# Causal attention and gated MLP: seven PSUM banks as one ring with a bank a turn, exps of 512 columns, and new orders of TensorE's work

## What is computed

```python
qkv = x @ w_qkv                                  # x: (8, 512, 128)
q, k, v = jnp.split(qkv, 3, axis=2)              # 16 heads of 8
att = jnp.einsum('bhtd,bhsd->bhts', q, k) / np.sqrt(D)
att = jnp.where(causal, att, -jnp.inf)
att = jax.nn.softmax(att, axis=-1)
out = jnp.einsum('bhts,bhsd->bhtd', att, v)
x = _layernorm(x + out)
h = jax.nn.silu(x @ wg.T) * (x @ wu.T)
x = _layernorm(x + h @ wd.T)
```

## Time and profile before

| what | value |
|---|---|
| median of 3 runs | 353.14 us (351.8 to 357.61) |
| the profiled execution's own time | 353.12 us |
| its span (first to last instruction) | 351.4 us |
| busy: PE, DVE, ACT, POOL | 95%, 84%, 61%, 51% of the span |
| mean granted clock of TensorE | 0.989 of full speed |

### The profile page before, as it was taken

One profiled execution on the slowest core, in us unless ns is written; L12 is line 12 of the kernel. 1 busy time (PEld: TensorE's weight loads), 2 busy tenths in 40 slices (PEclk: granted clock), 3 DMA queues, 4 the chain that ended last, 5 costly groups with the idle time before them and its releaser, 6 DMA issues. The chain is left out here.

```text
span 351.4 us, 9106 instructions
## 1 busy us (share of the span) xinstructions
PE 333.8 (95%) x2947; PEld 197.1 (56%) x2947; DVE 294.0 (84%) x1251; ACT 214.7 (61%) x277; POOL 178.4 (51%) x325
## 2 busy tenths in 40 slices
PE   7799999999999999999999999999999998999990
PEld 3444464556556555645564565456455544798980
DVE  7979778898899889889898998899898974867765
ACT  3402567777767768677777777776677784333320
POOL 8400334734654474357445534843434469787633
PEclk9999989999999999999999999999999999999997
DMA  5797242554265327624541653185100010002021
GB/s 155 288 296 250 62 123 64 197 171 123 62 245 174 109 73 261 168 73 169 198 121 34 245 147 110 41 288 165 49 2 5 5 34 1 3 30 62 30 62 60
DMA packets 33903, 41.75 MB, mean 119 GB/s; under 512 B 3136, under 2 KB 17472, under 8 KB 33856
## 3 DMA queue, kind: packets, MB, share of 16 engines
q1 hardware_dynamic: 33696, 40.91, 36.7%
q10 hardware_dynamic: 160, 0.26, 0.2%
HBM read 21.76 MB, written 18.87 MB: 116 GB/s over the span
## 5 line engine op out<-in xcount | busy, mean ns | idle before, releaser
L903 DVE CUSTOM_DVE_ANT_0 masked<-psum,mask 128x384 bf16<-128x384 f32 (+3 forms) x512 | 218.9, 487 | 30.7 <-PE psum L490 26.5
L803 ACT ACTIVATE pt<-psum 128x1024 f32<-128x1024 f32 x160 | 158.4, 1021 | 51.8 <-PE psum L473 51.2
L1082 POOL TENSOR_SCALAR_AFFINE_SELECT pt<-pt 128x512 f32<-128x512 f32 x128 | 79.6, 634 | 95.7 <-ACT pt L803 93.9
L490 PE MATMUL psum<-kx,qx 33*128 33x384 f32 (+3 forms) x512 | 91.8, 354 | 1.6 <-DVE nm L903 0.7
L513 PE MATMUL psum<-pt,vx 128*32 128x256 f32 (+2 forms) x1280 | 92.1, 388 | 1.1 <-ACT oT L817 0.8
L473 PE MATMUL psum<-qx,kx 35*128 35x384 f32 (+3 forms) x512 | 75.4, 342 | 0.5 <-ACT pt L803 0.5
L490 PEld LDWEIGHTS psum<-kx,qx 33*128 33x128 f32 x512 | 53.2, 186 | 37.8 <-DVE nm L903 18.6
L473 PEld LDWEIGHTS psum<-qx,kx 35*128 35x128 f32 x512 | 45.7, 185 | 29.0 <-issue 15.1
L513 PEld LDWEIGHTS psum<-pt,vx 128*32 128x32 f32 x1280 | 30.3, 109 | 38.3 <-issue 23.6
L903 DVE DVE_READ_ACCUMULATOR2_ANT nm<- 128x1 f32 x512 | 42.6, 83 | 0.0
L1070 POOL TENSOR_SCALAR nm_parts<-nm 128x16 fp32r<-128x16 f32 x32 | 6.6, 206 | 51.3 <-DVE nm L903 50.3
(11 more groups left out here) (64 smaller groups left out, 273.6 us busy)
## 6 DMA issues: line engine op xcount, KB each, us to landing
scr_q<-parts SPq DMA_DIRECT2D x16, 512.0 KB, 3.6
scr_k<-parts SPq DMA_DIRECT2D x16, 512.0 KB, 5.0
qx<-scr_q SPq DMA_DIRECT2D x64, 128.0 KB, 2.6
kx<-scr_k SPq DMA_DIRECT2D x62, 128.0 KB, 2.7
xa<-L_attn_x SPq DMA_DIRECT2D x8, 256.0 KB, 3.2
res<-L_attn_x SPq DMA_DIRECT2D x8, 256.0 KB, 2.8
out<-yo SPq DMA_DIRECT2D x8, 256.0 KB, 2.3
qx<-nm_T SPq DMA_DIRECT2D x64, 8.0 KB
```

The source lines that it names most:

```text
L490: last = pe.matmul(bank[:, col:col + width], qx[u][at:at + KM, 2 * g + hh // 2, P * i:P * i + P].bitcast(F32R), kx[u][at:at + KM, 2 * g + ...
L803: act.activation(pt[G % 2][:, 2 * s:2 * s + 2, :], pair_of("S", G, s), ACT.Exp, scale=SM_SCALE).then_inc(exp_done, 1)
L903: dve.tensor_tensor_reduce(masked[count % 4][:, 0:width], bank[:, col:col + width], mask[:, T - width:T], -1.0, 3.0e38, ALU.add, ALU.min, ...
L1082: pool.affine_select(out=blocks, in_=blocks, pattern=[[0, HG], [1, P]], compare_op=ALU.is_ge, fill=0.0, base=0, channel_multiplier=-1).the ...
```

## The change

The two score pairs and the three maxima banks become one ring of seven banks (0 to 6). One list, `BANK_TURNS`, holds every use in TensorE's order, a bank at a time; turn t may be written when the reader of turn t - 7 is done. An exp covers one bank (512 columns), so there are 320 of them and not 160, and `exp_done` and `st_full` count banks. V and X take a bank each. The orders in `group0` to `group3`, the list of `GROUP_TURNS` that has to agree with them, the order of the values' pieces, the place of VectorE's `normalise`, and ScalarE's list in its `for G` loop are new. The padding products inside groups (`add_zeros`) are gone from `group0` and `group1`.

```diff
@@ the list of bank uses: s = scores, m = maxima, n = turned maxima, o = turned output, q k v x = projections and input
+GROUP_TURNS = (
+    "s0 s1 m0 s2 s3 m1 m2 s4 m3 s5 m4 o n s6 m5 m6 s7 s8 s9 m7 m8 v x m9",
+    "m0 s0 s1 s2 s3 s4 m1 s5 m2 m3 m4 m5 s6 s7 m6 q s8 s9 m7 m8 n k m9",
+    "s0 s1 m0 m1 s2 m2 s3 n o s4 m3 s5 m4 m5 s6 m6 s7 m7 s8 m8 s9 m9",
+    "s0 s1 m0 s2 m1 s3 m2 s4 m3 s5 m4 n s6 m5 s7 s8 m6 m7 s9 m8 m9",
+)
+RING = 7
@@
-        st_ps = [psum[:, 0:2, :], psum[:, 2:4, :]]
-        mx_ps = [psum[:, 4, :], psum[:, 5, :], psum[:, 6, :]]
+        def bank_of(*turn):
+            return psum[:, BANK_TURNS.index(turn) % RING, :]
+        def bank_free(*turn):
+            t = BANK_TURNS.index(turn) - RING
@@ group1 on TensorE
             def group1(G):
                 V, M, b = G - 1, G + LAG, G // NG
-                values(V, "0a")
-                scores(G, 0)
-                scores(G, 1)
                 maxima(M, 0)
-                values(V, "1", "0b")
-                maxima(M, 2)
+                scores(G, 0, 1, 2, 3)
+                values(V, "0a", "1")
+                scores(G, 4)
+                maxima(M, 1)
+                scores(G, 5)
+                maxima(M, 2, 3, 4)
+                values(V, "0b", "3", "2")
+                maxima(M, 5)
+                scores(G, 6, 7)
+                maxima(M, 6)
+                project_q(b + 2)
+                scores(G, 8, 9)
+                maxima(M, 7, 8)
                 turn_negmax(G + 1)
...
+                project_k(b + 2)
+                maxima(M, 9)
@@ ScalarE
-            def exp_slot(G, s):
-                if G < GROUPS:
-                    act.wait_ge(st_full, SLOTS * G + s + 1)
+            def exps(G, *banks):
+                for n in banks:
+                    act.wait_ge(st_full, UNITS * G + n + 1)
                     if G > 1:
-                        act.wait_ge(pv_piece, PIECES * (G - 2) + pieces_read(G - 2, s))
-                    act.activation(pt[G % 2][:, 2 * s:2 * s + 2, :], pair_of("S", G, s), ACT.Exp,
-                                   scale=SM_SCALE).then_inc(exp_done, 1)
+                        act.wait_ge(pv_piece, PIECES * (G - 2) + pieces_read(G - 2, n))
+                    act.activation(pt[G % 2][:, n, :], bank_of("S", G, n), ACT.Exp, scale=SM_SCALE).then_inc(exp_done, 1)
...
+                elif n == 1:
+                    exps(G, 0, 1, 2, 3, 4, 5, 6, 7)
+                    copy_q_or_k(b + 2, 0)
+                    exps(G, 8, 9)
+                    copy_negmax(G + 1)
                     copy_out((G - 2) // 2)
-                if n == 0:
-                    copy_v_and_x(b + 1)
-                if n == 1:
                     copy_q_or_k(b + 2, 1)
```

More of the change, by code:

```diff
@@ L89, in score_turns @@
[L89 to L103, removed]
@@ L106, in maxima_turns, with bank_turns @@
[L106 to L115, removed]
+    return 1 + max(order.index(piece) for piece in (("0a", "0b") if n < HG else ("1", "3") if n < 2 * HG else ("2",)))
+GROUP_TURNS = (
[4 rows of a table added]
+)
+def bank_turns():
+    turns = [("X", 0), ("Q", 0), ("K", 0), ("V", 0), ("X", 1), ("Q", 1), ("K", 1), ("W", 0), ("W", 1), ("W", 2)]
+    turns += [("M", 0, k) for k in range(MX)]
+    turns += [("M", 1, 0), ("M", 1, 1), ("M", 1, 2), ("M", 1, 3), ("N", 0)] + [("M", 1, k) for k in range(4, 8)]
+    turns += [("S", 0, 0), ("S", 0, 1), ("M", 1, 8), ("M", 1, 9), ("S", 0, 2), ("S", 0, 3), ("M", 2, 0), ("M", 2, 1), ("N", 1)]
+    turns += [("S", 0, 4), ("S", 0, 5), ("M", 2, 2), ("M", 2, 3), ("S", 0, 6), ("S", 0, 7), ("M", 2, 4), ("M", 2, 5)]
+    turns += [("S", 0, 8), ("S", 0, 9)] + [("M", 2, k) for k in range(6, 10)]
+    for G in range(1, GROUPS - 1):
+        b = (G - 1) // NG
+        for turn in GROUP_TURNS[(G - 1) % NG].split():
+            if turn[0] == "s":
+                turns.append(("S", G, int(turn[1])))
+            elif turn[0] == "m" and G + LAG < GROUPS:
+                turns.append(("M", G + LAG, int(turn[1])))
+            elif turn == "n":
@@ L126, in attention_ffn @@
+    G = GROUPS - 1
+    return turns + [("S", G, n) for n in range(8)] + [("X1",), ("S", G, 8), ("S", G, 9), ("O", 2 * B - 2)]
+BANK_TURNS = bank_turns()
+RING = 7
 def attention_ffn(nc, x, w_qkv, w_gate, w_up, w_down, out):
@@ L407, in _ @@
         def _(pe):
[L408 to L411, removed]
             def take_bank(*turn):
@@ L464, in scores @@
                 u, g = G // NG % 2, G % NG
-                if G < GROUPS:
-                    if s == 0:
+                for n in banks:
+                    if n == 0:
                         pe.wait_ge(nm_loaded[G % 2], NM_LOADED * (G // 2 + 1))
[L468 to L476, removed]
+                    bank = take_bank("S", G, n)
+                    blocks = [(hh, j) for hh in range(HG) for j in range(NB) if key_block_place(hh, j)[0] == n]
+                    for hh, j in blocks:
+                        col, width, at = key_block_place(hh, j)[1], T - P * j, 64 * (hh % 2)
+                        last = pe.matmul(bank[:, col:col + width],
+                                         kx[u][at:at + KS, 2 * g + hh // 2, P * j:P * j + P].bitcast(F32R),
+                                         qx[u][at:at + KS, 2 * g + hh // 2, P * j:T].bitcast(F32R),
+                                         start=((hh, j) == blocks[0]), stop=((hh, j) == blocks[-1]), skip_group_check=True)
@@ L598, in group2 @@
-                scores(G, 3)
                 turn_out(half_of(G))
-                values(V, "2", "3")
+                scores(G, 4)
+                maxima(M, 3)
+                scores(G, 5)
+                maxima(M, 4, 5)
+                scores(G, 6)
+                values(V, "2")
                 maxima(M, 6)
-                values(V, "1")
-                scores(G, 4)
+                scores(G, 7)
+                maxima(M, 7)
+                scores(G, 8)
+                values(V, "0b", "1")
@@ L604, in group2 @@
                 maxima(M, 8)
+                scores(G, 9)
+                maxima(M, 9)
             def group3(G):
```

349 lines of the change are left out of this document (165 added, 184 removed).

## The result

The changed kernel takes 503.75 us (median of 5 runs, 501.03 to 506.5) where the kernel before takes 353.76: a ratio of 1.4285, 95% interval 1.4207 to 1.4362. The forecast was 342. The first part of the page of the changed kernel, the answer to the earlier trace rows: busy time, share and instructions of each engine.

The account below looks back on a forecast made before the run. VectorE was taken as the bound, needing 27.9 us of each 32.4 us batch. With waits of 0.65 and 2.3 a batch takes 30.85, over 7.25 batches: 353.1 - 11.2 + 0.4 = 342.3, said 342; range 329 to 354.

Parts of the forecast that it names:

- What bounds the kernel: Whole batch: VectorE works through, needing 27.9 us of 32.4 and losing 4.5 when not fed; TensorE could take 25.
- Point 3: Turned maxima at the end of group1: VectorE dry while group2's first score waits for copy and DMA, 2.3 us a batch.
- Point 1: Order and ring of seven, walked with VectorE always busy: it does not run dry in group2, group3 and group0.
- points 2: Start of group1: score bank 2 waits for the reduction of m8, leaving VectorE dry for 0.65 us.
- the sum: Whole kernel: batches of 30.85 us instead of 32.4, giving 342.3 us, said as 342; chance 0.50.
- Point 4: Exps of 512 on ScalarE: 20 more a batch cost 1.4 to 3.4 us, hidden by 8.4 us of idle time.
- Point 5: Start and end: nothing at the start; at the end ScalarE's later chain adds 0.4 us.
- B: Shared ring: ScalarE's lateness reaches VectorE, so no change, a batch of 32.4 us, 353 (348 to 358); chance 0.22.
- C: TensorE: single even and odd banks don't run together, up to 8 us more a batch, 365 in all; chance 0.13.
- D: End of group1: the wait for the turned maxima is covered, a batch is 28.55 us, 325 in all; chance 0.15.

Follow-up runs that it names:

- best2: Changed kernel with turned maxima and their copies early, products of zeros in first batch's group 0 and last two batches, output copied earlier in group 30; 341.87 us.
- b_512: Kernel before with each exp of 1024 columns done as two of 512, all waits as before; 354.05 us, beside 354.97 for the kernel before.
- a_pad2: Changed kernel with products of zeros ahead of its waits for turned maxima and their copy, the very first scores, and in first and last two batches; 392.98 us.
- b_late_pad: Kernel before with group 1's turn and copy late, group 2 beginning with scores, and 10 products of zeros ahead of that wait; 376.97 us.
- b_late: Kernel before with group 1's turn moved to the end, its copy behind the last exp, and group 2 beginning with scores; 424.14 us.
- best2_act: best2 with ScalarE's copies of the turned maxima put back behind exp 9 in group 0 and exp 8 in group 3; 414.54 us.
- a_early: Changed kernel with group 1's turn behind score bank 5 and ScalarE's copies of turned maxima behind exp 5 (exp 3 in group 2); 365.58 us.
- b_nopad: Kernel before without the padding that the change took out of groups 0 and 1; 364.13 us against 354.97.
- best1: a_early with eight products of zeros in the first batch's group 0 and the output copied ahead of exps 8 and 9 in group 30; 351.85 us.
- a_pad: Changed kernel with products of zeros ahead of the waits for turned maxima, 10 in group 2 and 8 in group 0 of each batch; 407.75 us.

## Why the prediction was wrong

- *What bounds the kernel: right at full clock.* VectorE's 27.9 us a batch and the 4.5 it loses fit what followed: best2 takes 30.9 us a batch with VectorE idle for 2.5 us before its reductions and not 3.6, and b_512 shows that ScalarE is not it.
- *Point 3, the wait: right in place and size.* 2.17 us idle on TensorE in the changed kernel, 2.25 on VectorE in a_pad2, 2.4 a batch in b_late_pad; the forecast was 2.3.
- *The step that failed: the price of that wait.* "Per batch VectorE then needs 27.9 + 0.65 + 2.3 = 30.85 us" takes every pace from rows at a clock of 1.00 and keeps them. But the wait stops the engine whose clock depends on what it does. b_late against b_late_pad: a wait that lasts 2.4 us a batch costs 35 to 47 us more over the kernel when it is not filled. In the changed kernel itself the clock is some 111 of the 150 us (a_pad2). No rival had this. The kernel before showed the hint: it issues products of zeros, 90 in all, in places where TensorE would have had little to do. I called them padding, and costed their removal and the new idle stretches at what they last.
- *Point 1, the walk: wrong for groups 0 and 3.* I followed the ring on TensorE and VectorE but not ScalarE's own order. In group 0, m7 takes the bank of the turned maxima, and their copy stands behind exp 9 (1.30 us in a_pad2); in group 3 the copy stands behind exp 8 and the next group's first score waits for its DMA (1.52 us). I had both at zero, and group 0's detour (1.09) and m9 (0.50) too. With points 2 (0.97 for 0.65) and 3, and the 27.9 of work, the waits listed come to 35.7 us a batch; measured are 36.7, where the sum had 30.85. The last 1.0 us these rows don't place. With the clock held, the change would still have been slower, 393 us.
- *The sum's 342 us came true for another kernel:* best2, which has no such wait, has 341.87. That it is the same number is chance: its batch of 30.9 us has no 2.3 in it for point 3, and loses it elsewhere (points 1 and 2).
- *Point 4, the exps: right*, 1.2 us a batch, hidden (b_512).
- *Point 5, the end: a wait left out.* In group 30 TensorE waits for the copy of the output, 2.2 us in the changed kernel and 1.5 in a_pad2. The sum had 0.4 for the end, for another reason.
- *Rivals:* B (ScalarE's lateness reaches VectorE through the ring) was the mechanism of 1.30 us in group 0, through a copy and not through exps' length. C (banks don't pair) did not happen: in the changed kernel's full-clock stretches even and odd banks start together (a scores and a maxima matmul both at 163.19 us). D did not happen.

## What to carry to other kernels

Where TensorE's granted clock is full in a kernel that needs TensorE for only part of the time (here an estimated 25 of 32.4 us a batch), that clock depends on the order of its work. A new wait of about 2 us with nothing issued was here followed by 10 us and more at half clock, so price the work behind it at half clock, not the wait at its length, or fill it with products of no use. Look also at stretches that are merely thin in work. When banks go into one ring, walk it with the static order of every reader: a small copy that stands late in one engine's list holds a bank that another engine's feeder needs. And keep what carries a result to another engine through a DMA (here 3.2 us from copy to use) as early as its data allow.

## What the runs showed of the hardware

- One TensorE wait of 2.14 us a batch was followed by 10.2 us at half clock (b_late), and one of 1.95 us by 17.0, with a second wait of 1.31 us inside them (best2_act). In best2 its waits for that DMA came to 1.0 us in three batches, and the clock was full until 337 us.
- A fall needs no wait of that length. In the changed kernel the first one, at 35 us, follows a wait of 1.02 us. In a_early at 49 us, b_nopad at 251 us and best1 at 245 us no wait of TensorE in the 8 us ahead is over 0.5 us, and products of zeros put there removed the falls of a_early and best1 (best1, best2). How little work is too little these runs don't measure.
- Half clock can last: a batch of the changed kernel took 57.3 us, with TensorE shown busy for 53.9 of them, and the clock did not come back in it. It came back 41 us later, for 10.2 us. What decides when it comes back these runs don't settle.
- Products of zeros count as work for the clock: a_pad against the change, 0.917 against 0.653, and b_late_pad against b_late, 0.97 against 0.825.
